# L2Max and L2Sum: TensorE waits once per tile for the signal of its own last product

## What is computed

```python
z = proj_s[src] + proj_t[dst]                  # feature @ W_s.T and feature @ W_t.T
z = jnp.where(z >= 0, z, NEG_SLOPE * z)
e = (z @ W_attn.T)[:, 0]                       # one score per edge
m = jax.ops.segment_max(e, src, num_segments=n)
e_exp = jnp.exp(e - m[src])
denom = jax.ops.segment_sum(e_exp, src, num_segments=n)
alpha = e_exp / denom[src]
msg = feature[src] * alpha[:, None]
agg = jax.ops.segment_sum(msg, dst, num_segments=n)
return agg @ W_fc.T + b_fc
```

## Time and profile before

| | |
|---|---|
| median of 3 runs | 6750.23 us |
| the profiled execution | 6752.3 us, its span 6750.5 us |
| mean granted TensorE clock | 0.812 |
| TensorE matmul, busy | 4675.7 us, 69% |
| VectorE, busy | 3880.6 us, 57% |
| GpSimd, busy | 3474.4 us, 51% |
| ScalarE, busy | 2148.6 us, 32% |
| L2Max | from 3417 to 4068 us |
| L2Sum | from 4135 to 4780 us |

### The profile page before, as it was taken

One profiled execution on the slowest core, in us unless ns is written; L12 is line 12 of the kernel. 1 busy time (PEld: TensorE's weight loads), 2 busy tenths in 40 slices (PEclk: granted clock), 3 DMA queues, 4 the chain that ended last, 5 costly groups with the idle time before them and its releaser, 6 DMA issues. The chain is left out here.

```text
span 6750.5 us, 92101 instructions
## 1 busy us (share of the span) xinstructions
PE 4675.7 (69%) x21663; PEld 3026.9 (45%) x21663; DVE 3880.6 (57%) x14947; ACT 2148.6 (32%) x7478; POOL 3474.4 (51%) x3739
## 2 busy tenths in 40 slices
PE   3566674747895555638767774778778478888858
PEld 3223333737882222424345553555567233336635
DVE  8676543130016666351578877777532667778875
ACT  0000000212231222302344444444223188874421
POOL 3636665446635666456556663666122166656610
PEclk9776656869996776955689997999788699989978
DMA  1133335546745666013155555777456166664410
GB/s 47 48 98 91 91 92 159 185 143 218 232 149 151 181 181 175 14 45 103 49 151 162 148 145 152 237 237 236 133 150 170 45 173 171 172 154 141 140 44 20
DMA packets 526133, 916.95 MB, mean 136 GB/s; under 512 B 100305, under 2 KB 382880, under 8 KB 517168
## 3 DMA queue, kind: packets, MB, share of 16 engines
q0 software_dynamic: 170800, 477.35, 26.0%
q1 hardware_dynamic: 294378, 305.07, 14.5%
q10 hardware_dynamic: 60438, 128.64, 6.0%
HBM read 739.33 MB, written 171.37 MB: 135 GB/s over the span
## 5 line engine op out<-in xcount | busy, mean ns | idle before, releaser
L999 PE MATMUL bank<-small 128*125 128x256 f32 x1660 | 763.2, 587 | 472.3 <-DVE small L966 239.9
L947 POOL DMA_INDIRECT small<-tabA,idxD x830 | 809.9, 976 | 441.0 <-issue 187.2
L999 PEld LDWEIGHTS bank<-small 128*125 128x125 f32 x1660 | 368.1, 268 | 866.6 <-issue 469.5
L978 DVE TENSOR_TENSOR big<-big,bank 125x256 f32 x830 | 347.1, 418 | 490.4 <-PE bank L999 312.6
L2506 POOL DMA_INDIRECT small<-tabC,idxD x415 | 394.5, 951 | 343.2 <-issue 124.5
L2559 PE MATMUL bank<-small 128*125 128x512 f32 x830 | 474.6, 656 | 127.1 <-issue 104.0
L2548 ACT ACTIVATE small<-cst,small 128x128 f32<-128x128 f32 x1660 | 532.2, 388 | 94.0 <-issue 40.0
L1342 DVE COPY small<-bank 128x256 f32<-128x256 f32 x176 | 74.5, 424 | 834.5 <-PE bank L1382 423.2
L2277 POOL DMA_INDIRECT big<-tabB,idxD x415 | 394.6, 951 | 300.1 <-PE bank L2340 133.6
L2091 POOL DMA_INDIRECT small<-tabT,idxS x415 | 396.5, 955 | 284.5 <-PE bank L1989 141.2
L781 POOL DMA_INDIRECT recs<-pkS,rowS x391 | 383.8, 982 | 249.4 <-issue 100.2
(11 more groups left out here) (463 smaller groups left out, 11371.0 us busy)
## 6 DMA issues: line engine op xcount, KB each, us to landing
small<-eaS SPq DMA_DIRECT2D x830, 128.0 KB
big<-in_L_w ACTq DMA_DIRECT2D x56, 1024.0 KB
eaS<-small SPq DMA_DIRECT2D x415, 128.0 KB
big<-in_L2f_w ACTq DMA_DIRECT2D x64, 512.0 KB
ytab<-small ACTq DMA_DIRECT2D x176, 128.0 KB
big<-rowsS SPq DMA_DIRECT2D x52, 256.0 KB
small<-rowsD SPq DMA_DIRECT2D x52, 256.0 KB
small<-tabA,idxD POOLq DMA_INDIRECT x830
```

Source lines behind the costliest of these rows:

```text
L947: g.indirect_dma_start(out=self.gb[k % self.RG], out_offset=None, in_=K.tabA, in_offset=row_index(K.idxD, k)).then_inc(*self.got.up(k))
L978: v.tensor_tensor(rows, rows, K.bank[k % 4][0:PT, 0:D], ALU.add).then_inc(*self.added.up)
L999: p.matmul(self.K.bank[k % 4][0:PT, 0:D], self.oh[k % self.RO][:, 0:PT], self.gb[k % self.RG], start=True, stop=True).then_inc(*self.summe ...
```

## The change

After its last product of a tile, TensorE now waits until this product's own signal has been raised, before it goes on to the next tile. In L2Max that is the signal `field` of L2160, in L2Sum `summed` of L2340.

```diff
@@ -2158,6 +2158,7 @@
                 p.matmul(b[:, 0:128], self.oh[j % 5], self.dg[j % 5], start=True, stop=False)
                 p.wait_ge(*self.hole.n(j + 1))
                 p.matmul(b[:, 0:128], self.no[j % 5], pr.bigI, start=False, stop=True).then_inc(*self.field.up)
+                p.wait_ge(*self.field.n(j + 1))
 
 
 class L2Combine:
@@ -2338,6 +2339,7 @@
                 if j >= 4:
                     p.wait_ge(*self.added.n(j - 3))
                 p.matmul(K.bank[4 + j % 4][0:PT, 0:D], self.oh2[j % self.RO][:, 0:PT], self.gb[j % self.RB][:, DP:DP + D], start=True, stop=True).then_inc(*self.summed.up)
+                p.wait_ge(*self.summed.n(j + 1))
```

## The result

The changed kernel takes 6871.79 us (median of 4 runs, 6862.06 to 6889.78), against 6746.15 us for the kernel before on the same chip (4 runs, 6729.89 to 6758.26): the ratio is 1.0186, 95% interval 1.0168 to 1.0205. That is +126 us where +509 was forecast. The direction is right, the size is a quarter of the forecast. The time lies inside the range of 6790 to 7420 us, but in the part that the range took in for the second case, prompt signals; the first case alone began at 6938.

A forecast was written before the change was run, and what follows sets the result against it. TensorE's signals were taken to be held while gathers are issued, its run-ahead keeping the pace bearable. L2Max 158, L2Sum 326 and table loads 25 sum to 509 us on 6752, rounded to 7260 us; range 6790 to 7420.

The forecast's parts named there:

- second case: Both passes: TensorE's signals come promptly, even while gathers run; still slower, near 6805 us; chance 0.08.
- first case: Both passes: TensorE's signals are held while gathers are issued; 6938 to 7422 us; chance 0.81.
- step 2: Smaller bunches: one gather per round in L2Sum, 2.34 us a tile, +326 us; L2Max 1.95 us a tile, +158 us.
- Step 1: TensorE's wait: restart 0.29 us per tile; with prompt signals 1.49 us a tile in L2Max, 1.63 in L2Sum, -33 and +31 us.
- Step 3: Table loads L211, 50 of about 1.1 us, lie bare behind the wait, partly covered by slack: +25 us, at most 55.
- Steps 4 and 5: VectorE, ScalarE and transfers cost nothing; a lower TensorE clock is not charged, some 35 us kept at the upper end.
- Signals come promptly: Rival: signals prompt since TensorE is in step with them; restart and bare loads give +53 us, 6805 us; chance 0.08.
- The other side: Rival: run-ahead itself holds the signals and the restart is hidden; 1.30 and 1.44 us a tile, about 6650 us; chance 0.06.
- right: Signs: L2Max near 810 us, L2Sum near 970; gathers singly or in pairs; L1987's idle time up by some hundreds of us.
- wrong: Signs: gathers 0.30 us apart throughout, VectorE reading products within 0.1 us of their end, passes at or below 650 us.

The follow-up runs named there:

- plain_again: Kernel before with both passes' gathers replaced by SyncE's plain transfers of fixed row blocks, on a late chip: 6433.36 us, ratio 0.9510.
- before_again: The kernel before, unchanged, run again for a trace on a late chip: 6763.20 us.
- onesig: Kernel before with one TensorE signal per tile instead of two and no self-wait: 6678.24 us, ratio 0.9984.
- plain_self: Kernel before with gathers replaced by plain transfers of fixed row blocks, plus the change, on a prompt chip: 6128.60 us, ratio 1.0259 to before.
- skip_load: The changed kernel without the wait ahead of tiles that load table offsets, in both passes: 6740.79 us, ratio 1.0075 to the kernel before.
- load_only: Kernel before with the wait added only ahead of the 25 table loads of each pass, on a prompt chip: 5972.31 us, ratio 1.0003.
- load_b: Repeat of load_only against the kernel before in another group, again on a prompt chip: 5971.89 us, ratio 1.0002.

## Why the prediction was wrong in size

*What bounds the kernel: right.* The late signals and their tie to the gathers are shown by plain_again; the rounds stay in before_again and onesig. Wrong was that all signals are held while gathers are issued and come only once GpSimd is quiet: see step 2.

*Step 1, the wait itself: mis-sized.* The restart was put at 0.29 us, from a dispatch behind VectorE's signal. Behind TensorE's own it is 0.14 us, and a tile in lockstep takes 1.44 to 1.48 us in L2Sum (GpSimd's spacing above), not 1.63. plain_self shows the step by itself: without the 25 loads of 1.1 us a tile takes (576 - 27.5) / 415 = 1.32 us in L2Max and (641 - 27.5) / 415 = 1.48 in L2Sum, against 1.49 and 1.63.

*Step 2, smaller bunches: this is the step that failed.* It forecast 2.34 us a tile for L2Sum (+326) and 1.95 for L2Max (+158). The waits on ordinary tiles cost 18 and 33 us (skip_load), below even its bounds of +104 and +62. It took the release of a signal as a fixed time after the last gather, 2.05 us, and so had to hold every product that ended 1.34 us after a gather. The product above that ended 1.21 us after one had its signal out within 0.14 us, and more than half of the signals of L1989 were prompt (231 and 237 of 415). The traces show otherwise: the stalled reads come 1.48 us after the last start where gathers are 1.44 us apart, 1.67 to 1.70 after a pair, 1.93 to 1.95 after three and 2.05 after four. The forecast of L2Max failed less, since pairs do form there; but their tail is 3704.88 - 3702.98 = 1.90 us, not 2.18, which makes 1.57 a tile and not 1.72; what L2Max lost beside the loads is in its rounds of one and of three. A tail read from rounds of three and four was carried over to rounds of one and two.

Over whole passes, the median stalled read behind a pair comes 1.66 us after the last start in L2Max after the change (102 reads), behind three 1.93 before it (73), behind four 2.10 in L2Sum before it (49), and behind gathers 1.44 us apart 1.50 (95 reads, some of them at 2.05). The series looks like a backlog that gathers 1.25 us apart build up and gathers 1.44 us apart do not. But the eight reads behind pairs in L2Sum before the change come at 1.95, and in the rows of L2Sum above a product that ended 1.21 us after a gather was prompt and one that ended (4506.24 + 0.59) - 4505.66 = 1.17 us after the next was held. What decides stays open: the three runs that were to tell the backlog from other readings fell on chips with prompt signals.

*Step 3, the table loads: mis-sized the other way.* 51 to 59 us (skip_load against the full change) instead of 25, about the bound of 55. The slack that was to cover them belonged to step 2's 2.34 us a tile and did not exist. load_only and load_b show, on prompt chips alone, that without the lockstep a load behind the wait costs nothing.

*Steps 4 and 5: right to leave out.* The clock is 0.93 and 0.98, and TensorE's busy time in L2Max rose by 518 - 508 = 10 us, which bounds what the clock cost there. The transfers' share of time fell.

*The rivals.* "Signals come promptly", 6805 us, gave nearest to the measured time, but by two errors that cancel: lockstep alone takes 576 + 641 us, 79 less than the 1296 of before and not 53 more, and signals are still held a part of the time (144 and 48 us). That it came nearest is luck. The other side, 6650 us, had the lockstep right: 1.30 and 1.44 us a tile against 1.32 and 1.48 in plain_self. It failed because its first condition, prompt signals, holds in part only on this chip. Of the sum, 33 + 18 + 59 = 110 us were measured (in windows), against 158 + 326 + 25 = 509.

*What would show it.* Of the rows named for "right" some appeared in L2Max: pairs with 0.96 to 0.99 us of idle time, and VectorE's idle time up from 94.4 to 132.5 us. The decisive ones did not: the passes take 722 and 691 us, and L1987's idle time is up by 85 and 3 us. L2Sum shows the sign named for step 1 alone, a start of L1987 every 1.44 to 1.48 us where nothing is held. The rows named for "wrong" did not appear either.

No kernel here that keeps the gathers is faster than before by a measurable amount; the change is best left out, or made to wait for the tile before, which costs nothing.

## What to carry to other kernels

A wait on one's own last instruction costs the restart and everything behind it in the queue that used to run under cover: look for the long instruction there (here a register load of 1.1 us, 50 times), and wait one iteration later instead. A delay that is read from a bunched rhythm belongs to that rhythm; before carrying it to another one, look in the trace for the nearest case with that spacing. And where a pass is slowed by something that comes and goes, work out the new pace both with and without it: the floor here, lockstep alone, was 576 and 641 us (plain_self), 196 us below the passes of the changed kernel, where the forecast lay 388 us above its time.

## What was not expected of the hardware

- TensorE's signals are late only beside GpSimd's gathers, on late chips: 45 of 415 signals of L1989 in L2Max come within 0.1 us before the change, 415 of 415 without gathers (plain_again), and VectorE's reads wait 77.5 us and 4.5 us for them.
- How late differs from group to group, each on another chip as far as the record tells: the same kernel takes 6693 to 6765 us in three and 5969 to 5971 us in three others, 11 to 12% less, at equal length of the gathers (0.95 us) and of VectorE's work. On prompt chips the passes run at GpSimd's pace, 1.25 us a gather (load_b, whose time is that of before), and the same change costs 2.76% instead of 1.86%.
- TensorE restarts 0.14 us after the (modelled) end of a product whose own signal it waits for, where that signal is prompt.
